# Attention: the second row tile's causal mask moved from TensorE to VectorE, and the ring of PSUM banks in a new order

## What is computed

```
q, k = rope(x @ wq), rope(x @ wk)      # 32 heads, 8 key heads, 16 wide, 256 rows
scores = q @ k.T / 4                   # per batch and head
scores = where(causal, scores, -inf)
out = softmax(scores) @ v              # then @ wo
```

## Time and profile before

| | us |
|---|---|
| median of 3 runs | 2930.53 |
| lowest and highest | 2928.91, 2933.16 |
| the profiled execution, its own time | 2930.81 |
| its span | 2929.1 |
| mean granted TensorE clock, share of full speed | 0.982 |

### The profile page before, as it was taken

The page is one execution under the profiler, slowest core; times in us unless marked ns, Lnnn a source line. Parts: engine busy times, 40 slices in busy tenths (PEclk is TensorE's granted clock), DMA queues, the critical chain, the costliest instruction groups (busy, mean ns, idle before and its releaser), DMA issues.

```text
span 2929.1 us, 45881 instructions
## 1 busy us (share of the span) xinstructions
PE 2793.4 (95%) x16150; PEld 2283.9 (78%) x16150; DVE 1236.7 (42%) x2152; ACT 877.9 (30%) x1697; POOL 838.8 (29%) x1306
## 2 busy tenths in 40 slices
PE   6989999988999939999999999999999999999998
PEld 6865555556666529999999999999999999999997
DVE  6756777747888833332232232132133133133111
ACT  1126666641555512221121121122122122122110
POOL 4546776631166641101101111011021021011010
PEclk9999999999999969999999999999999999999999
DMA  3101222242122223221122032032033033022010
GB/s 109 43 1 31 48 45 48 55 92 87 68 84 75 77 83 106 91 86 64 51 92 75 26 108 83 15 109 87 12 108 101 11 100 104 14 90 85 26 47 21
DMA packets 97078, 194.68 MB, mean 66 GB/s; under 512 B 22126, under 2 KB 23758, under 8 KB 96800
## 3 DMA queue, kind: packets, MB, share of 16 engines
q1 hardware_dynamic: 75072, 131.77, 15.1%
q0 software_dynamic: 21856, 60.73, 6.6%
HBM read 148.77 MB, written 38.94 MB: 64 GB/s over the span
## 4 chain that ended last, share of the span: by engine, by line
PE 62%; DMA 0%; POOL 0%; DVE 0%; issue 0%; ACT 0%; DVEq 0%; POOLq 0%
PE ex_hid L1775 31%; PE ex_acc L102 10%; PE ex_acc L103 10%; PE ex_acc L104 10%; PE ex_xb L1745 1%; DMA ex_ys<-xn_dram,ex_slot_gather 0%; POOL out_dram L1627 0%; POOL ex_ys L1607 0%; DVE ex_ys L1688 0%; POOL ex_xg L1592 0%; DMA ex_ys<-slot_table_dram 0%; PE ex_acc L1745 0%; DVE ex_h0l L1696 0%; ACT ex_h0h L1655 0%; DVE ex_xT0l L1671 0%
## 5 line engine op out<-in xcount | busy, mean ns | idle before, releaser
L1696 DVE SCALAR_TENSOR_TENSOR ex_h0l<-ex_hid,ex_h0h 128x640 fp32r<-128x640 f32 x128 | 105.5, 824 | 682.8 <-ACT ex_h0h L1655 682.8
L1696 DVE SCALAR_TENSOR_TENSOR ex_h1l<-ex_hid,ex_h1h 128x640 fp32r<-128x640 f32 x128 | 105.4, 824 | 602.9 <-ACT ex_h1h L1655 602.3
L1655 ACT ACTIVATE ex_h0h<-ex_hid 128x640 fp32r<-128x640 f32 x128 | 90.1, 704 | 734.5 <-PE ex_hid L1775 734.5
L1655 ACT ACTIVATE ex_h1h<-ex_hid 128x640 fp32r<-128x640 f32 x128 | 90.1, 704 | 729.8 <-PE ex_hid L1775 729.8
L654 DVE TENSOR_REDUCE at_nb<-at_ring 128x2 f32<-128x512 f32 (+1 forms) x384 | 246.8, 685 | 121.1 <-PE at_ring L760 120.9
L1597 POOL COPY ex_gi<-ex_slot_gather 128x1 int32 (+1 forms) x82 | 15.3, 187 | 918.2 <-PE ex_xb L1745 913.3
L102 PE MATMUL ex_acc<-ex_w_h,ex_h1h 128*128 128x512 f32 x640 | 254.8, 398 | 0.0
L102 PE MATMUL ex_acc<-ex_w_h,ex_h0h 128*128 128x512 f32 x640 | 253.4, 396 | 0.0
L103 PE MATMUL ex_acc<-ex_w_l,ex_h0h 128*128 128x512 f32 x640 | 250.3, 391 | 0.0
L103 PE MATMUL ex_acc<-ex_w_l,ex_h1h 128*128 128x512 f32 x640 | 250.2, 391 | 0.0
L104 PE MATMUL ex_acc<-ex_w_h,ex_h1l 128*128 128x512 f32 x640 | 249.8, 390 | 0.0
(11 more groups left out here) (273 smaller groups left out, 5665.2 us busy)
## 6 DMA issues: line engine op xcount, KB each, us to landing
ex_raw<-in_w_tiles_dram SPq DMA_DIRECT2D x256, 256.0 KB, 2.8
x_in<-in_x_dram SPq DMA_DIRECT2D x32, 256.0 KB, 2.7
act<-at_raw SPq DMA_DIRECT2D x128, 64.0 KB
at_recb<-o_rec_dram SPq DMA_DIRECT2D x16, 512.0 KB
k<-in_x_dram SPq DMA_DIRECT2D x32, 256.0 KB, 2.7
cx_ctx<-in_ctx_dram SPq DMA_DIRECT2D x16, 512.0 KB, 3.8
out_dram<-cx_res SPq DMA_DIRECT2D x16, 512.0 KB, 2.8
xn_dram<-cx_prob SPq DMA_DIRECT2D x16, 512.0 KB, 2.8
```

The lines of the kernel that those rows point to most:

```text
L1655: act.activation(h[f % 2][0][:], hid[:, :, 0:HB], ACT.Relu).then_inc(sm["h_hi"], 1)
L1696: dve.scalar_tensor_tensor(h[f % 2][1][:], hid[:, :, 0:HB], 0.0, f32(h[f % 2][0][:]), ALU.max, ALU.subtract).then_inc(sm["h_lo"], 1)
```

## The change

The tile `mask` grows from 128 x 128 to 128 x 256: its left half is zero, and its right half is the triangle of before. The first row tile (parts 0 and 1) keeps its mask matmul and its `TENSOR_REDUCE`. For the second row tile (parts 2 to 5) the two mask matmuls of a part go. In their place DVE runs, for each of a piece's two heads, a `tensor_tensor_reduce` that adds the mask to 256 scores, multiplies by -1, writes the result back into the bank and keeps the minimum, which is the negated maximum.

The ring becomes one turned bank and then a pair of scores, six times: `k`, `m`, `qa`, `qb`, `qc`, `qd`. PE's order inside a part becomes `shifted`, the turned bank, `score`, `values`. ACT copies `qa`, `qb` and `qd` ahead of the exponentials of parts 2, 3 and 5. DVE copies `k` behind the two maxima of part 0 and `qc` behind those of part 4.

```diff
-        TURNS = ("s0", "s1", "m", "qa", "s2", "s3", "s4", "s5", "qb", "qc", "s6", "s7", "s8", "s9", "qd", "k", "s10", "s11")
+        TURNS = ("k", "s0", "s1", "m", "s2", "s3", "qa", "s4", "s5", "qb", "s6", "s7", "qc", "s8", "s9", "qd", "s10", "s11")
...
                 for p in range(6):
+                    if p >= 2 and p != 4 and within(h + 1, 0, HALVES):
+                        name = sorted(QUERIES)[p - 2]
+                        keep_q(h + 1, (2 * q + e + 1) % 4, name, bank(e, name))
...
-                    if p == 0 and within(h - 1, 0, HALVES):
+                    if p == 1 and within(h - 1, 0, HALVES):
                         act.wait_ge(sm["m_turned"], ONE + h)
...
-                    if p % 2 == 0 and within(h + 1, 0, HALVES):
-                        name = ("qa", "qb", "qd")[p // 2]
-                        keep_q(h + 1, (2 * q + e + 1) % 4, name, bank(e, name), p // 2)
...
+                            wait_apart(dve, sm["scores"], PIECES * h + n + 1, passed_dve)
+                            width, qb, heads = S, 1, range(p // 2 * 2 - 2, p // 2 * 2)
+                            for c, a in enumerate(heads):
+                                y = x[:, c * width:c * width + width]
+                                m = dve.tensor_tensor_reduce(y, y,
+                                                             t["mask"][:, S - width:S], -1.0, LARGEST, ALU.add, ALU.min,
+                                                             nb[e][:, r, p % 2, a, qb:qb + 1])
+                            m.then_inc(sm["maxima"], 1)
+                    if p == 0 and within(h + 1, 0, HALVES):
+                        keep_k(h + 1, (2 * q + e + 1) % 4, bank(e, "k"))
+                    if p == 4 and within(h + 1, 0, HALVES):
                         keep_q(h + 1, (2 * q + e + 1) % 4, bank(e, "qc"))
-                    if p == 4 and within(h + 1, 0, HALVES):
-                        keep_k(h + 1, (2 * q + e + 1) % 4, bank(e, "k"))
...
+                        m = pe.matmul(banks[r][:, c, :], qs[i][rows, p % 2, n, width - P:width],
+                                      ks[i][rows, p % 2, 0:width], start=True, stop=p >= 2, skip_group_check=True)
+                        if p >= 2 and c == len(heads) - 1:
+                            m.then_inc(sm["scores"], 1)
+                if p < 2:
+                    for r in range(2):
+                        pe.matmul(banks[r][:], t["identb"][:], t["mask"][:, P:S].unsqueeze(1).to_broadcast([P, REP, P]),
+                                  start=False, stop=True, skip_group_check=True).then_inc(sm["scores"], 1)
...
                     if live_d:
                         shifted(h - 2, i_d, p)
+                    if p == 0 and within(h + 1, 0, HALVES):
+                        turn_k(h, j, e)
+                    if p == 1 and within(h - 1, 0, HALVES):
+                        turn_m(h, e)
+                    if p >= 2 and within(h + 1, 0, HALVES):
+                        turn_q(h, e, sorted(QUERIES)[p - 2])
                     if live_s:
                         score(j, q, e, p)
```

More of the change, by code:

```diff
@@ L38 @@
 MASKED = -1e30
+LARGEST = 3e38
 ONE = 1
@@ L159, in _ @@
             pool.wait_ge(mask_set, ONE + 2)
-            pool.affine_select(out=t["mask"][:], in_=t["mask"][:], compare_op=ALU.is_ge, fill=MASKED, base=0,
+            pool.affine_select(out=t["mask"][:, P:S], in_=t["mask"][:, P:S], compare_op=ALU.is_ge, fill=MASKED, base=0,
                                pattern=[[-1, P]], channel_multiplier=1)
@@ L565, in _, with keep_q @@
         def _(act):
-            def keep_q(h, i, name, x, n):
+            def keep_q(h, i, name, x):
                 act.wait_ge(sm["q_turned"], ONE + 4 * h + 1 + sorted(QUERIES).index(name))
@@ L578, in first @@
             def first():
-                for n, name in enumerate(("qa", "qb", "qd")):
-                    keep_q(0, 0, name, bank(1, name), n)
+                for name in ("qa", "qb", "qd"):
+                    keep_q(0, 0, name, bank(1, name))
             def step(j, w, q, e):
@@ L651, in step @@
                             n = 2 * p + r
[L652 to L657, removed]
+                            x = bank(e, f"s{n}")
+                            if p < 2:
+                                dve.wait_ge(sm["scores"], ONE + PIECES * h + n + 1)
+                                dve.tensor_reduce(nb[e][:, r, p % 2, :, 0], x[:].rearrange("p (h k) -> p h k", h=REP),
+                                                  AX.X, ALU.max, negate=True).then_inc(sm["maxima"], 1)
+                                continue
+                            wait_apart(dve, sm["scores"], PIECES * h + n + 1, passed_dve)
[9 more added lines that the diff above has]
+                    if p == 4 and within(h + 1, 0, HALVES):
                         keep_q(h + 1, (2 * q + e + 1) % 4, bank(e, "qc"))
-                    if p == 4 and within(h + 1, 0, HALVES):
-                        keep_k(h + 1, (2 * q + e + 1) % 4, bank(e, "k"))
                     if e == 1 and p == 5 and within(j - 2, 0, B):
@@ L1795, in decoder_layer @@
         t["identb"] = s.sb("identb", [P, P], BF16)
-        t["mask"] = s.sb("mask", [P, P], BF16)
+        t["mask"] = s.sb("mask", [P, S], BF16)
         t["ones"] = s.sb("ones", [P, P])
```

## The result

The changed kernel takes 3125.7 us against 2931.9 for the kernel before (medians of four runs each): a ratio of 1.066, with a 95% interval of 1.064 to 1.068. It is slower by 194 us where 59 were forecast, and lies far above the range.

What follows compares the result with a forecast made beforehand. PE was taken to bound the attention loop: 11.45 us of work plus waits of 1.47, 1.72 and 0.16 made a half 14.80 us against 12.90. 31 x 1.90 = 59 us on 2930.8 gave 2990, range 2952 to 3065.

Steps and rivals of the forecast that it cites:

- The prediction's last sign of being wrong: PE's waits for the two copies short or missing, or the shifted scores beginning to wait for ACT instead.
- The sizes of the two waits: PE stands 1.47 us for DVE's copy of `k` in part 1, 1.72 us for that of `qc` in part 5.
- The price a: DVE's cost of one 256-element instruction with its read-out, start to start: 0.44 us, bounds 0.44 and 0.65.
- The wait of 0.16 us in part 3: In part 3, `s7` waits for DVE's reading of `s4`: 1.03 us less 0.87 of PE's filling work.
- I cost them at nothing: ACT's copies ahead of exponentials and POOL's earlier stacking of keys get cover, both busy some 70%: 0 us.
- The sum: PE's work and three waits make a half of the attention loop 14.80 us against 12.90, 59 us in all.
- PE's work of 11.45 us: PE's work in a half: 12.55 us unheld, less 1.10 for four pairs of mask matmuls taken away.
- a bound below the sum: PE's work with the cheapest start-to-start of each piece: 0.8 us less a half, giving 2965 us.
- The clock: Rival: PE's clock falls in ten halves of the attention loop, 8 us each, 80 us on top, 3070; chance 0.10.
- the argument against it: Earlier low PE shares lasted some 10 us in a row; here each half has dense matmuls between the waits.
- No overlap on DVE (a = 0.65): Rival: each DVE instruction waits for the last to finish; a half 17.07 us, 130 us more, 3061; chance 0.13.
- Faster: Rival: the two copies don't hold PE, only the mask matmuls count; 34 us less, 2897; chance 0.06.

Runs made afterwards that it cites:

- e1: The changed kernel with DVE's copies of `k` and `qc` moved ahead of the maxima of parts 0 and 4: 2964.2 us.
- e8: The changed kernel with only DVE's copy of `qc` moved ahead of the maxima of part 4; that of `k` stays behind: 3032.4 us.
- e6: e5 with ACT's copies of turned queries put back behind the two exponentials of their parts: 2951.3 us.
- e4: The changed kernel with each shifted matmul of parts 1 and 5 run four more times ahead of the one that counts: 3042.4 us.
- e5: e1 with PE turning its bank ahead of the shifted scores in every part: 2923.8 us.
- e7: The changed kernel with only DVE's copy of `k` moved ahead of the maxima of part 0; that of `qc` stays behind: 3106.8 us.
- e10: e5 with DVE's copy of `qc` put back behind the maxima of part 4: 2988.8 us.
- e2: The changed kernel's new order, but with the kernel before's mask matmuls on PE and one 512-element reduction for the maxima: 3066.1 us.

## Why the prediction was wrong

**What bounds the kernel, and the sign: right.** PE's pace in the loop set the time, and the forecast sign and mechanism held: two copies of DVE stand where PE waits for them. e1 shows it, by moving only these. The prediction's last sign of being wrong came too: the shifted scores began to wait for ACT, though beside the two waits and not in their place.

**The sizes of the two waits: right.** Part 1: 1.92 us to `s2` forecast, 1.90 measured (e8). Part 5: 2.59 us from the shifted scores to `s10` forecast, 2.66 measured (406.92 to 409.58). The second was right by errors against each other. DVE's timeline has the parts:

```profile
407.27 0.43 DVE L663 CUSTOM_DVE_ANT_0 at_ring<-at_ring,mask 128x256 f32<-128x256 f32 x1 [0.81 <-PE at_ring L767]
...
408.77 0.68 DVE L631 TENSOR_SCALAR at_qs<-at_ring 128x512 fp32r<-128x512 f32 x1
```

The price a was 0.38 and not 0.44, so four heads cost 1.50 for 1.76. But DVE began 0.35 us after the start of the shifted scores, where 0.09 was taken from a score with a mask matmul behind it, and PE went on 0.13 after the copy's end (409.45 to 409.58), where 0.06 was taken. The wait of 0.16 us in part 3 did not appear: PE goes from the turn to the scores in 0.59 us (403.55 to 404.14).

**Copies and exponentials of ACT, "I cost them at nothing": wrong.** A busy share of 70% is no cover for a place. In part 3 the shifted scores wait for an exponential that now stands behind ACT's copy: 1.0 us a half. ACT's timeline shows the order:

```profile
401.98 0.60 ACT L570 ACTIVATE at_qs<-at_ring 128x512 fp32r<-128x512 f32 x1 [4.92 <-PE at_ring L737]
402.48 1.08 ACT L596 ACTIVATE at_pT<-at_st 128x512 f32<-128x512 f32 x2
```

ACT sat idle until the bank that it copies was turned (401.29 to 401.95 on PE), while the shifted scores for the exponential had run from 400.79 to 401.36. The sum named 0.6 as the price if the cover were gone, and left it out. No run puts the exponential back in front with all else as in the changed kernel; e6 did so only where PE turns first.

**PE's work of 11.45 us: too small.** It kept each piece's price and took away the masks. In e1, free of the copies' waits and of both other waits (1.00 and about 0.37), a half is 13.68 - 1.37 = 12.31: about 0.9 us more. The same matmuls cost more from start to start in the new order; why was not shown. I gave a bound below the sum here and none above it.

These two would add 1.9 us. But 0.2 of the longer work lies in parts 1 and 5, under the waits for the copies, and the 0.16 of part 3 was not there. So the half at full clock is 16.3 us and not 14.8, as e4 measures it; 1.5 x 31 = 47 us.

**The clock: given a chance of 0.10, and priced right by luck.** The price was 80 us, from a fall in ten of 31 halves at 8 us each. e4 measures 83, but the clock fell once in every half of the middle of the loop, at 2.6 us a half on average (18.99 - 16.43). The step that failed is the argument against it, that dense matmuls between the waits would hold the clock. The earlier trace rows showed the full clock only over a stretch just before it fell, and that was no evidence that it holds. The Trainium skill (TensorE: Matmul & The Clock Gate, "A second HAM failure mode: psum-queue depth-cycling") described short idles between groups that make the clock swing; this case's trace agrees, with 1.00 and 0.51 in neighbouring stretches of 10 us.

Together: 2990 + 47 + 83 = 3120, against 3125.7. Both added terms are read from e4, so this shows that they account for the loss, and is no forecast.

**No overlap on DVE (a = 0.65): out.** A read-out of 0.14 us and the next instruction start at the same time, 0.08 us before the end of the one ahead. **Faster: rightly unlikely as built.** Without the two waits (e1) it still was not faster; it took PE's order of e5 as well.

## What to carry to other kernels

When a ring gets a new order, write down for each use whose reader it waits for and what stands ahead of that reader in its engine's queue: two copies of 0.68 us, behind maxima instead of ahead of them, cost 162 us here. A wait of 1.2 to 1.7 us, repeated in every half, was not priced by its length alone; where the trace of before can't show that the clock holds through it, the half clock belongs in the main case. A busy share of 70% doesn't hide an instruction that is put ahead of one that somebody waits for: in the changed kernel ACT was busy for only 143 of 300 us, and PE waited for it in part 3.

## What the runs showed of the hardware

The read-out of DVE's accumulator, 0.14 us long, starts together with the next instruction, and the pair takes 0.38 us from start to start. A lone instruction of 256 elements was estimated at 0.35 from the earlier trace rows, so by that estimate the read-out adds 0.03. More matmuls made the kernel faster: 16 repeated ones a half brought the clock from 0.81 to 1.00 and saved 83 us. How much clock is lost did not follow the length of the wait alone: 1.67 us in part 5 went with a mean of 0.77 in e7, 1.47 us with 0.93 in e10, and 0.93 and 1.20 us together with 0.94 in e2. Within one run the same wait of 1.47 us (e10) went with a full clock in some halves and a fall in others. What decides between these was not settled.
